# Decoder layer on one core: x turned by VectorE in 32x32 blocks while it is mixed, in place of transposes on TensorE

## The reference

```
qkv = x @ w_qkv
q, k, v = jnp.split(qkv, 3, axis=-1)          # 8 heads of 64
fq, fk, fv = fft(q), fft(k), fft(v)
kv = jnp.cumsum(fk * fv, axis=1)              # over the tokens
vals = ifft(kv * conj(fq)).real
x = layernorm(x + vals @ w_out)
```

## Time and profile before

| | |
|---|---|
| three runs | 966.97, 967.0 and 970.75 us; median 967.0 us |
| span of the profiled execution | 964.6 us |
| the median minus this span | 2.4 us |
| TensorE busy | 917.6 us, 95% |
| VectorE busy | 666.7 us, 69% |
| ScalarE, GpSimd busy | 376.8 and 337.8 us |
| mean granted clock of TensorE | 0.982 of full speed |

### The profile page before, as it was taken

The page is one execution under the profiler, slowest core; times in us unless marked ns, Lnnn a source line. Parts: engine busy times, 40 slices in busy tenths (PEclk is TensorE's granted clock), DMA queues, the critical chain, the costliest instruction groups (busy, mean ns, idle before and its releaser), DMA issues.

```text
span 964.6 us, 14638 instructions
## 1 busy us (share of the span) xinstructions
PE 917.6 (95%) x4476; PEld 754.5 (78%) x4476; DVE 666.7 (69%) x1128; ACT 376.8 (39%) x1403; POOL 337.8 (35%) x310
## 2 busy tenths in 40 slices
PE   5898999999999999999779999999999999999987
PEld 4784888888888888888668788888888888888775
DVE  3363466665656565555667888979889798887957
ACT  3152120101010111102287566656567565666610
POOL 2000243232222232324236434444443444433733
PEclk9998999999999999999979999999999999999999
DMA  5944201221203020203423122131222203120021
GB/s 179 326 148 172 90 1 52 80 80 52 104 28 127 3 87 1 88 23 116 134 81 102 25 79 73 40 113 24 89 63 78 75 21 122 30 89 21 17 77 44
DMA packets 72346, 76.02 MB, mean 79 GB/s; under 512 B 38567, under 2 KB 40871, under 8 KB 72303
## 3 DMA queue, kind: packets, MB, share of 16 engines
q1 hardware_dynamic: 72303, 75.49, 24.4%
HBM read 52.60 MB, written 22.87 MB: 78 GB/s over the span
## 4 chain that ended last, share of the span: by engine, by line
PE 41%; DVE 4%; ACT 2%; issue 2%; POOL 2%; POOLq 0%; DVEq 0%
PE shared_ps L74 31%; PE score_ps L74 4%; PE shared_ps L1146 4%; ACT probs L1352 2%; PE shared_ps L1109 1%; PE shared_ps L1179 1%; POOL probs L1501 1%; DVE score_ps L1658 1%; DVE xT_lo L1615 0%; DVE x_and_res L1704 0%; DVE top_s L1663 0%; DVE pT_lo L1642 0%; POOL x_and_res L1516 0%; DVE y L1682 0%; DVE w_o_lo L1825 0%
## 5 line engine op out<-in xcount | busy, mean ns | idle before, releaser
L1352 ACT ACTIVATE probs<-score_ps,top_s 128x77 f32<-128x77 f32 x512 | 159.0, 359 | 36.9 <-DVE top_s L1663 36.9
L1352 ACT ACTIVATION_READ_ACCUMULATOR probs<-score_ps,top_s 128x1 f32 x512 | 122.9, 240 | 0.0
L1501 POOL TENSOR_TENSOR probs<-probs,per_total 128x616 f32<-128x616 f32 x64 | 82.7, 1309 | 65.9 <-DVE per_total L1670 65.7
L1494 POOL TENSOR_TENSOR rstd<-ve,half_power 128x1 f32<-128x1 f32 x64 | 42.4, 662 | 157.1 <-DVE ve L1693 152.5
L722 POOL TENSOR_TENSOR vals<-qs_prod 128x512 f32<-128x512 f32 x32 | 41.1, 1296 | 127.1 <-DVE qs_prod L804 127.1
L713 POOL TENSOR_TENSOR mix_rstd<-mix_ve,half_power 128x1 f32<-128x1 f32 x32 | 22.0, 688 | 175.4 <-DVE mix_ve L823 175.4
L1658 DVE COPY_PREDICATED score_ps<-hidden,masked 128x616 f32<-128x616 int32 x64 | 66.2, 1034 | 11.6 <-PE score_ps L74 11.6
L1359 ACT ACTIVATE pT_hi<-shared_ps 103x512 fp32r<-103x512 f32 (+1 forms) x96 | 54.7, 612 | 46.0 <-PE shared_ps L1146 45.5
L672 ACT ACTIVATE v_sb<-v_ps 128x512 f32<-128x512 f32 x32 | 18.9, 594 | 133.9 <-PE v_ps L74 133.9
L679 ACT ACTIVATE qT_hi<-vals 128x512 fp32r<-128x512 f32 x32 | 19.4, 631 | 122.3 <-POOL vals L722 106.2
L1642 DVE TENSOR_TENSOR pT_lo<-shared_ps,pT_hi 103x512 fp32r<-103x512 f32 (+1 forms) x96 | 64.5, 684 | 0.0
(11 more groups left out here) (218 smaller groups left out, 2660.1 us busy)
## 6 DMA issues: line engine op xcount, KB each, us to landing
x_tok<-in_x SPq DMA_DIRECT2D x8, 1024.0 KB, 5.9
x_res<-in_x SPq DMA_DIRECT2D x8, 1024.0 KB, 8.0
x_between<-mix_x SPq DMA_DIRECT2D x32, 256.0 KB, 2.0
x<-x_between SPq DMA_DIRECT2D x8, 1024.0 KB, 5.5
x_tok<-x_between SPq DMA_DIRECT2D x8, 1024.0 KB, 5.7
out<-y_out SPq DMA_DIRECT2D x32, 256.0 KB, 2.0
wqkv_sb<-in_w_qkv SPq DMA_DIRECT2D x4, 768.0 KB, 7.8
keys_split<-w_q_hi SPq DMA_DIRECT2D x8, 154.0 KB, 5.4
```

The source lines that it names most:

```text
L1352: nc.scalar.activation(probs[:, t % 2, j * KEYS:(j + 1) * KEYS], score_ps[:, g, k * KEYS:(k + 1) * KEYS], ACT.Exp, bias=top[:, t % 2, j:j ...
L1494: nc.gpsimd.tensor_tensor(rstd[:, n:n + 1], ve[:, n:n + 1], half_power[:], ALU.pow).then_inc(rstd_ready, 1)
L1501: nc.gpsimd.tensor_tensor(p, p, per_total[:, t % 2, h * heads:(h + 1) * heads].unsqueeze(2) .to_broadcast([P, heads, KEYS]), ALU.mult).the ...
```

## The change

x is loaded in another layout, in which VectorE can turn it. Partition 32a+c (a from 0 to 3, c from 0 to 31) of x_tok now holds the tokens 32u+c for all 16 values of u, and of each the features 128a to 128a+127. This needs four transfers of 32 partitions, whose pieces are 512 bytes long (`load_blocks`); before, it was one transfer of 128 partitions with pieces of 2048 bytes. VectorE's transpose turns each 32x32 block by itself, so one instruction over 16 blocks (b fixed) gives all 512 tokens of the features 128a+32b+r on partition 32a+r, written to x_turned in SBUF, which holds two chunks. A chunk therefore is another set of 128 features than before, and the rows of w_qkv are loaded in the same order (`weight_rows`). ScalarE and VectorE split from x_turned (SBUF) instead of xT_ps (PSUM). TensorE does no transposes of x in the mixing; the wait for the loaded x moves from TensorE to VectorE. The bank xT_ps stays as spare_ps for the last batch.

```diff
+def load_blocks(sp, tile, rows, sem):
+    src = rows.rearrange("(u c) (a j) -> a c u j", c=BLOCK, a=P // BLOCK)
+    for a in range(P // BLOCK):
+        dst = tile[a * BLOCK:(a + 1) * BLOCK, :, :].rearrange("c t (k j) -> c (t k) j", j=P)
+        sp.dma_start(dst, src[a]).then_inc(sem, 16)
+
+def weight_rows(w, b):
+    return w.rearrange("(a b r) n -> b a r n", a=P // BLOCK, r=BLOCK)[b]
...
-            sp.dma_start(x_first[:], ins["x"][0].rearrange("(t p) d -> p t d", p=P)).then_inc(x_loaded, 16)
+            load_blocks(sp, x_first, ins["x"][0], x_loaded)
...
-                sp.dma_start(x_tok[half][:], x[i].rearrange("(t p) d -> p t d", p=P)).then_inc(x_loaded[half], 16)
+                load_blocks(sp, x_tok[half], x[i], x_loaded[half])
...
# TensorE, step
-                for c, (s, h) in enumerate([(1, 0), (1, 1), (0, 0)]):
-                    if has_next:
-                        turn(i + 1, 1 - half, c)
+                for s, h in [(1, 0), (1, 1), (0, 0)]:
                     project(i, half, s, 0, h)
-                if has_next:
-                    turn(i + 1, 1 - half, 3)
...
# ScalarE
-                nc.scalar.activation(xT[half][0][:, c, :], bank[:], ACT.Copy).then_inc(x_hi, 1)
+
+                if c == 0:
+                    wait_reuse(act, q_filled, (i - 1) * 4)
+                nc.scalar.activation(xT[half][0][:, c, :], x_turned[:, c % 2, :], ACT.Copy).then_inc(x_hi, 1)
...
# VectorE
+            def turn(i, half, c):
+                if c == 0:
+                    dve.wait_ge(x_loaded[half], i_loads(i, half))
+
+                wait_reuse(dve, x_lo, nth(i, NC, c - 2))
+                wait_reuse(dve, x_hi, nth(i, NC, c - 2))
+                nc.vector.transpose(x_turned[:, c % 2, :].rearrange("p (u c) -> p u c", c=BLOCK),
+                                    x_tok[half][:].rearrange("p t (k b c) -> p (t k) b c", b=NC, c=BLOCK)[:, :, c, :]
+                                    ).then_inc(xT_filled, 1)
...
-                turned(0)
+                if has_next:
+                    turn(i + 1, 1 - half, 0)
+                    turn(i + 1, 1 - half, 1)
                 times_k(i, 0, 0)
-                turned(1)
+                if has_next:
+                    split_x(i + 1, 1 - half, 0)
+                    turn(i + 1, 1 - half, 2)
                 times_k(i, 0, 1)
-                turned(2)
+                if has_next:
+                    split_x(i + 1, 1 - half, 1)
+                    turn(i + 1, 1 - half, 3)
                 scan(i, 0)
-                turned(3)
+                if has_next:
+                    split_x(i + 1, 1 - half, 2)
+                    split_x(i + 1, 1 - half, 3)
                 times_q(i, 0, 0)
...
-            for c in range(NC):
-                split_x(0, 0, c, first_banks[c])
+            turn(0, 0, 0)
+            turn(0, 0, 1)
+            split_x(0, 0, 0)
+            turn(0, 0, 2)
+            split_x(0, 0, 1)
+            turn(0, 0, 3)
+            split_x(0, 0, 2)
+            split_x(0, 0, 3)
```

More of the change, by code:

```diff
@@ L67, in v_pieces @@
                 yield j, c, a - at, a - j * KEYS, b - a
+BLOCK = 32
+def load_blocks(sp, tile, rows, sem):
[5 more added lines that the diff above has]
+    return w.rearrange("(a b r) n -> b a r n", a=P // BLOCK, r=BLOCK)[b]
 def split_matmuls(nc, out, pieces):
@@ L160, in _ @@
             sp.dma_start(fwd[:], ins["dft_forward"]).then_inc(fwd_loaded, 16)
-            sp.dma_start(wqkv_sb[:, 0, :], ins["w_qkv"][0:P, :]).then_inc(qkv_loaded[0], 16)
+            sp.dma_start(wqkv_sb[:, 0, :], weight_rows(ins["w_qkv"], 0)).then_inc(qkv_loaded[0], 16)
             for n in range(NKEY):
@@ L176, in _ @@
                     sp.wait_ge(wv_lo_ready, NC)
-                    sp.dma_start(wqkv_sb[:, n, :], ins["w_qkv"][n * P:(n + 1) * P, :]).then_inc(qkv_loaded[n], 16)
+                    sp.dma_start(wqkv_sb[:, n, :], weight_rows(ins["w_qkv"], n)).then_inc(qkv_loaded[n], 16)
             for n, (at, size) in enumerate(tiles):
@@ L479, in mix_tokens @@
         q_ps = [ps(f"q_ps{h}", [P, S]) for h in range(2)]
-        xT_ps = ps("xT_ps", [P, S])
+        spare_ps = ps("spare_ps", [P, S])
+        x_turned = sb("x_turned", [P, 2, S])
         out_ps = ps("out_ps", [P, D])
-        first_banks = [xT_ps, k_ps[0], k_ps[1], q_ps[0]]
         next_banks = [k_ps[0], k_ps[1], q_ps[0], q_ps[1]]
-        last_banks = [out_ps, xT_ps, v_ps[0], v_ps[1]]
+        last_banks = [out_ps, spare_ps, v_ps[0], v_ps[1]]
         x_loaded = [hand.x_loaded, sem("x_loaded1")]
@@ L556, in _ @@
         def _(pe):
[L557 to L570, removed]
             def project(i, half, s, p, h):
@@ L620, in step @@
                     project(i, half, s, 1, h)
-            for c in range(NC):
-                turn(0, 0, c, first_banks[c])
             step(0, 0, True, False)
@@ L663, in _, with split_x @@
         def _(act):
-            def split_x(i, half, c, bank=xT_ps):
+            def split_x(i, half, c):
                 act.wait_ge(xT_filled, nth(i, NC, c))
-                nc.scalar.activation(xT[half][0][:, c, :], bank[:], ACT.Copy).then_inc(x_hi, 1)
+                if c == 0:
+                    wait_reuse(act, q_filled, (i - 1) * 4)
+                nc.scalar.activation(xT[half][0][:, c, :], x_turned[:, c % 2, :], ACT.Copy).then_inc(x_hi, 1)
             def copy_v(i, p, h):
@@ L693, in _ @@
             for c in range(NC):
-                split_x(0, 0, c, first_banks[c])
+                split_x(0, 0, c)
             step(0, 0, True, False)
@@ L763, in _, with i_loads, split_x @@
         def _(dve):
-            def split_x(i, half, c, bank=xT_ps):
+            def i_loads(i, half):
+                return ((i - half) * 8 + 16) * (P // BLOCK)
+            def turn(i, half, c):
[6 more added lines that the diff above has]
+                                    ).then_inc(xT_filled, 1)
+            def split_x(i, half, c):
                 dve.wait_ge(x_hi, nth(i, NC, c))
-                nc.vector.tensor_tensor(xT[half][1][:, c, :], bank[:], xT[half][0][:, c, :].bitcast(F32),
+                nc.vector.tensor_tensor(xT[half][1][:, c, :], x_turned[:, c % 2, :], xT[half][0][:, c, :].bitcast(F32),
                                         ALU.subtract).then_inc(x_lo, 1)
@@ L833, in step @@
             def step(i, half, has_next, has_last):
-                def turned(c):
-                    if has_next:
-                        split_x(i + 1, 1 - half, c)
-                turned(0)
+                if has_next:
+                    turn(i + 1, 1 - half, 0)
+                    turn(i + 1, 1 - half, 1)
                 times_k(i, 0, 0)
-                turned(1)
+                if has_next:
+                    split_x(i + 1, 1 - half, 0)
+                    turn(i + 1, 1 - half, 2)
                 times_k(i, 0, 1)
-                turned(2)
+                if has_next:
+                    split_x(i + 1, 1 - half, 1)
+                    turn(i + 1, 1 - half, 3)
                 scan(i, 0)
-                turned(3)
+                if has_next:
+                    split_x(i + 1, 1 - half, 2)
+                    split_x(i + 1, 1 - half, 3)
                 times_q(i, 0, 0)
```

## The result

| | before | after |
|---|---|---|
| median of the runs | 967.0 us (965.7 to 970.8) | 976.5 us (974.4 to 978.9) |
| time over before, 95% interval | | 1.0082 to 1.0117 |
| span of the profiled execution | 964.6 us | 975.6 us (its own time 977.5) |
| first issue in the mixing / in the attention | 86.22 / 475.46 us | 105.30 / 486.34 us |
| mean granted clock | 0.982 | 0.963 |

The change makes the kernel slower by about 9.5 us, where 960.1 us was forecast, with a range from 956.0 to 966.5. The two first issues divide the time. The preparation became 19.1 us longer, the mixing 8.2 us shorter (389.24 and 381.04 us), and the attention stayed (489.14 and 489.26 us): 19.1 - 8.2 + 0.1 = 11.0 us of span.

A forecast was written before the change was run, and what follows sets the result against it. TensorE, busy all the time at full clock, was taken to bound the mixing. From 967.0 us, -12.2 (transposes) + 1.5 (stall) + 1.9 (start) + 1.9 (clock) = -6.9 gave 960.1 us, range 956.0 to 966.5.

The forecast's parts named there:

- the paragraph on loads: DMA loads of x, the residual and w_qkv: all covered or unchanged, so no cost.
- TensorE's gain: Mixing: 28 groups of four transposes at 0.436 us each leave TensorE, -12.2 us.
- VectorE's price for a turn: VectorE's transpose of 128x512 float32: 0.60 us start to start, like the subtraction, with ends 0.55 and 1.22.
- The stall at r_added: TensorE's second back projection waits for the residual's addition on VectorE: 0.25 us in each of six steps, +1.5 us.
- The third turn: VectorE's turn behind split 0 in a step: ends 3.17 us after a k matmul, half 1 comes at 3.24, just covered.
- The start: Start of mixing: batch 0's turns and splits on VectorE and ScalarE delay TensorE's first v matmul, +1.9 us.
- The clock: Start of mixing: TensorE idles 7.4 us and then runs at half clock, +1.9 us, ends 0 and 3.
- The loads of x: Four transfers in place of one: 1 MB in 11.8 us, covered in steps and at the start, no cost.
- The rivals on the price of a turn: A turn costs VectorE what a scan does, 1.22 us; gain given back at r_added, 968 us; chance 0.13.
- VectorE as the bound: Rival: a turn takes 2.4 us and VectorE bounds each step, +21, 988 us; chance 0.05.
- late loads of x: Rival: 1 MB in small pieces takes over 16 us, residual late every step, 966 to 972 us; chance 0.05.
- GpSimd and the subtraction: Rival: splits with both inputs in SBUF wait out GpSimd passes in six steps, 7.7 us more, 967.8; chance 0.03.

The follow-up runs named there:

- E2: The kernel before with only w_qkv loaded in the permuted row order by the change's four transfers: 986.6 us, 1.0193 of before.
- E1: The whole change, with w_qkv brought in the same row order by transfers into 32 partitions each: 959.9 us, 0.9936 of before.
- E6: E1 with VectorE turning chunk 3 of x twice in each step that turns: 964.4 us, 0.9974 of before.
- E5: E1 with 20 useless matmuls keeping TensorE busy while batch 0 is turned at the mixing's start: 956.9 us, 0.9900 of before.
- E8: E7 with the four loads of w_qkv chunks 1 to 3 issued behind key stores 5 to 8: 955.0 us, 0.9883 of before.
- E9: E7 with chunk 3 of w_qkv loaded together with chunk 0 at the start: 949.6 us, in a second series 948.3 us.
- E10: The kernel before with only chunk 3 of w_qkv loaded at the start behind chunk 0: 964.6 us, 0.9969 of before.
- E7: E1 with batch 0 of x turned and split in the preparation: 951.3 us, 0.9847 of before; in a second series 952.1 us.

## Why the prediction was wrong

- **The step that failed** stands in the paragraph on loads: "The new row order of w_qkv has the same 6 KB pieces. No cost." Bytes and pieces are the same, but a transfer also has a shape. The term of 0 measured +19.1 us (E2: +20.6 by itself; E1 takes out 17.0). No row of the preparation shows anyone waiting for the loads themselves. The key stores, which share their engines, were late, and ScalarE, VectorE and TensorE hang on those. None of the rivals had a late transfer in the preparation. The rows to judge it by were there to be read: TensorE already stood 2.76 us for VectorE, so this stretch had no slack for slower transfers.
- **TensorE's gain**, -12.2 us: right. Between the same two matmuls of a step lie 8.63 us where 9.50 lay, 0.87 less for two groups. The sum of the mixing is -12.2 + 1.8 (start) + 2.0 (clock) = -8.4 us, and the two traces give -8.2.
- **VectorE's price for a turn**, 0.60 from start to start: measured 0.64 (205.02 to 205.66). The upper end of 1.22 was too cautious. The estimate from the Trainium skill, "VectorE: DVE Perf Modes", section "The three transpose paths", was 1.24 us; the measurement is half of it, and decides.
- **The stall at r_added**, +1.5 us: it did not come. TensorE needs the result 8.63 us after the last k matmul, as forecast to the hundredth (211.24 - 202.61), but it is there after 8.33, not after 8.67. From half 1's start to the addition 7.22 us pass, where 7.54 were added up. Part of the difference was hidden in the old stretch: its split 3 began at 188.73, when ScalarE's copy of 188.10 had ended, and VectorE had stood some 0.2 us for it without a row that says so. I had counted that as work. The third turn was just covered, as forecast: it would have let VectorE go on at 202.98, and k's half 1 came at 203.04. E6 shows how thin the rest of the slack is.
- **The start**, +1.9: measured +1.8. **The clock**, +1.9: measured 10 x 0.43 - 10 x 0.233 = 2.0 in the change, 2.5 by E5.
- **The loads of x**: right. Batch 1's 1 MB was there 7.8 us after the first of its four issues, and a part lands in 5.1 us (median); nothing waits in a step. Only batch 1's first turn waited 2.2 us for its data, with no one behind it.
- The rivals on the price of a turn, on VectorE as the bound and on late loads of x did not occur: TensorE waits for VectorE once in the mixing, at the start.
- **GpSimd and the subtraction.** In the step shown no subtraction is long (0.68 us), so GpSimd held nothing up there. But the prediction looked at step 2 alone. In step 1 GpSimd splits W_q with a subtraction of its own, and one of VectorE's falls beside it. Before and after:

```profile
132.26 5.05 POOL L752 TENSOR_TENSOR w_q_lo<-x,w_q_hi 128x512 fp32r<-128x512 f32 x4
133.68 0.69 DVE L766 TENSOR_TENSOR xT_lo<-xT_ps,xT_hi 128x512 fp32r<-128x512 f32 x1 [6.60 <-ACT xT_hi L666]
```

```profile
153.40 5.51 POOL L750 TENSOR_TENSOR w_q_lo<-x,w_q_hi 128x512 fp32r<-128x512 f32 x4
156.46 1.29 DVE L778 TENSOR_TENSOR xT_lo<-x_turned,xT_hi 128x512 fp32r<-128x512 f32 x1
```

With one input in PSUM the subtraction took 0.69 us beside GpSimd; with both in SBUF it took 1.29, and GpSimd's four took 0.46 longer. In each run with the change the longest of these subtractions takes 1.28 to 1.29 us. So what the rival describes is there, once and not six times; it is read from the rows, and no run tests it by itself. The 0.6 us used up the slack of that step: its second back projection started 0.31 us behind the matmul before it (166.03 and 166.34) in place of 0.23.
- That E1 comes to 959.9 us where 960.1 was forecast is partly luck: it loses 2.1 us in the preparation that the sum did not have, and has no stall. The 2.4 us between span and median is no constant either: it is 0.9 in the change (976.5 and 975.6) and 3.6 in E1 (959.9 and 956.3).

The remaining 2.1 us of E1 lie in the same wait and in the half clock behind it, but why the wait is longer is open. E8, E9 and E10 show that this stretch is sensitive to what is in transfer between 28 and 52 us, so the other partition of the loads (four of 576 KB in place of three of 768 KB, one of them a store later) is a likely cause; it was not tried alone.

## What to carry to other kernels

When a change rewrites the access pattern of a transfer, look at its outermost dimension as well as at its bytes and pieces, and write it so that the partitions come first: a transfer that covers 128 partitions as 4 groups of 32 ran on 4 engines, and transfers of 32 partitions each brought the DMA share back to 1. A DMA share stuck at 0.25 or 0.13 beside a queue full of work is the sign, and putting the slow transfer on another queue hardly helped (2.7 of 19.1 us). And a change that touches one stage must be checked in the stage that loads its data: here the stage that was changed gained what had been forecast.

## What the runs showed of the hardware

- In the stretches shown a DMA engine moved 23 to 26 GB/s, with few engines at work or all: 98 to 101 GB/s at a share of 0.24 to 0.26, 52 at 0.13, 368 at 1.01. It is no constant: in E1's row of 36 to 38 us it is 228 GB/s at 0.99, 14 each.
- The transpose of 128x512 float32 (16 blocks of 32x32 in each group of 32 partitions) took VectorE 0.71 us, hardly more than a subtraction of the same size, though it reads with jumps.
- A subtraction of VectorE with both inputs in SBUF took 1.29 us in place of 0.68 beside a GpSimd subtraction; with one input in PSUM it took 0.69 at the same place.
- The same idle time of 2.43 us at the same place left TensorE's clock at half for six matmuls in E7's profile and at full in that of E7's and E9's second series. Also the attention, untouched by all this, took 486.4 and 486.5 us in two profiles (E9's second, E1) and 489.1 to 490.2 in the twelve others; in E1's, its second 40 us ran at a clock of 1.00, in E5's at 0.96. Differences of 2 to 3 us between single profiles, in the stages behind, are of that kind.
